# A Mamba block between two ternary FFNs on one core: the first pass's silu from a tanh on ScalarE and a product on VectorE

## What is computed

```
x = x + 0.5 * ffn(layernorm(x))       # ffn: ternary weights times their mean absolute value, plus a bias
x = x + mamba(layernorm(x))
x = x + 0.5 * ffn(layernorm(x))       # the same weights

mamba(x):
  u, z  = split(x @ W_in.T)           # 1024 features each
  u     = silu(causal convolution of u along the tokens, 4 taps, plus conv_b)
  x_dbl = u @ W_xproj.T               # 64 columns for dt, 16 for B, 16 for C
  dt    = softplus(x_dbl[:, :64] @ W_dt.T + b_dt)
  h[t]  = exp(dt*A) * h[t-1] + dt * B[t] * u[t]      # 16 states a feature, A = -exp(A_log)
  y     = sum over states of h*C + u * Dskip
  out   = (y * silu(z)) @ W_out.T
```

## Time and profile before

| | us |
|---|---|
| median of 3 runs (2982.8 to 2990.77) | 2988.41 |
| the profiled execution | 2993.49 |
| its span in the trace | 2991.6 |
| first pass in it (the second pass's first load is at 1093.77) | about 1094 |
| DVE busy / PE busy / ACT busy over the span | 2483.3 / 2457.8 / 1943.3 |

### The profile page before, as it was taken

How to read it: one execution, slowest core, us unless ns; L and a number is a source line. 1 busy time by engine, 2 the same in 40 slices (tenths; PEclk the granted TensorE clock), 3 DMA queues, 4 the chain that set the end, 5 groups by cost and what they waited for, 6 DMA issues and landing times.

```text
span 2991.6 us, 42858 instructions
## 1 busy us (share of the span) xinstructions
PE 2457.8 (82%) x12448; PEld 1413.9 (47%) x12448; DVE 2483.3 (83%) x3261; ACT 1943.3 (65%) x3457; POOL 1921.5 (64%) x1705
## 2 busy tenths in 40 slices
PE   3577999899998726788889888888888888889887
PEld 1233444444443315555555555555555555555553
DVE  5565666767666649999999999999999999999991
ACT  2233766756765666677777767767777767777772
POOL 1112222222221138899989989989989989999983
PEclk8788999999998857799999999999999999999998
DMA  5454233233232263352352352353352352343330
GB/s 206 155 205 168 78 128 135 78 128 121 92 128 107 79 214 117 92 131 69 112 132 68 99 140 74 99 132 82 98 133 76 102 135 72 106 119 87 105 76 35
DMA packets 175016, 337.66 MB, mean 113 GB/s; under 512 B 41696, under 2 KB 91104, under 8 KB 174496
## 3 DMA queue, kind: packets, MB, share of 16 engines
q1 hardware_dynamic: 160928, 284.23, 28.8%
q0 software_dynamic: 13824, 50.34, 8.8%
HBM read 174.61 MB, written 109.58 MB: 95 GB/s over the span
## 4 chain that ended last, share of the span: by engine, by line
POOL 28%; DVE 13%; issue 12%; PE 5%; DMA 3%; ACT 1%; POOLq 1%; SPq 0%; DVEq 0%; ACTq 0%
POOL dbu L1055 22%; DVE h L1279 9%; DVE y L1292 3%; PE p_g L1402 2%; PE p_g L1411 1%; PE p_ht L1368 1%; POOL o L1100 1%; DMA y<-y_part 1%; POOL carry L1066 1%; POOL y L1075 1%; POOL y L1090 1%; POOL x L1094 1%; DMA dt_<-dt_scratch 1%; POOL dbu L1060 1%; DMA dtu_<-dtu_scratch 1%
## 5 line engine op out<-in xcount | busy, mean ns | idle before, releaser
L1279 DVE TENSOR_TENSOR_SCAN h<-p_da,dbu 128x512 f32<-128x512 f32 x1024 | 1189.0, 1206 | 44.7 <-ACT p_da L1161 21.9
L1055 POOL TENSOR_TENSOR dbu<-dtu_,bb 128x1024 f32<-128x1024 f32 x512 | 1205.3, 2385 | 4.7 <-DMA dtu_<-dtu_scratch 4.1
L1161 ACT ACTIVATE p_da<-dt_,neg_a 128x255 f32<-128x255 f32 x2048 | 886.5, 467 | 400.3 <-DVE h L1279 377.5
L1368 PE MATMUL p_ht<-ident,h 128*128 128x128 f32 x4096 | 596.6, 305 | 157.9 <-DVE h L1279 156.7
L1368 PEld LDWEIGHTS p_ht<-ident,h 128*128 128x128 f32 x4096 | 534.6, 159 | 250.5 <-issue 111.2
L1292 DVE SCALAR_TENSOR_TENSOR y<-p_ht,ct,y 128x1024 f32<-128x1024 f32 x400 | 505.9, 1265 | 4.9 <-PE p_ht L1368 4.8
L714 PE MATMUL p_u<-xz,wu 128*128 128x512 f16 x1536 | 351.4, 386 | 10.8 <-DVE xz L508 9.2
L1402 PE MATMUL p_g<-wo,tokt 128*128 128x512 f16 x1536 | 355.2, 389 | 1.6 <-ACT tokt L1193 1.6
L70 POOL TENSOR_TENSOR small<-small,consts 128x1 f32<-128x1 f32 x96 | 71.1, 740 | 441.4 <-DVE small L63 441.4
L1411 PE MATMUL p_g<-wz,xz 128*128 128x512 f16 x1536 | 345.2, 381 | 0.0
L363 POOL TENSOR_TENSOR late<-dt,u 128x512 f32<-128x512 f32 x64 | 81.7, 1276 | 378.0 <-DVE dt L561 378.0
(11 more groups left out here) (120 smaller groups left out, 3053.7 us busy)
## 6 DMA issues: line engine op xcount, KB each, us to landing
y<-y_part POOLq DMA_DIRECT2D x96, 512.0 KB, 5.8
bb<-b_scratch SPq DMA_DIRECT2D x128, 256.0 KB, 3.5
xin<-in_x SPq DMA_DIRECT2D x32, 512.0 KB, 5.5
x_scratch<-x SPq DMA_DIRECT2D x32, 512.0 KB, 4.8
xz_scratch<-xz SPq DMA_DIRECT2D x16, 1024.0 KB, 6.0
y_scratch<-late SPq DMA_DIRECT2D x32, 512.0 KB, 5.1
dt_scratch<-dt SPq DMA_DIRECT2D x64, 256.0 KB, 2.1
dtu_scratch<-late SPq DMA_DIRECT2D x64, 256.0 KB, 2.4
```

The source lines that it names most:

```text
L1055: nc.gpsimd.tensor_tensor(state[:, 4 * f:4 * f + 4, :], dtu[:, 4 * f:4 * f + 4, :], bb[n // NB % 2][:, n % NB:n % NB + 1, :].to_broadcast( ...
L1161: ins_ = nc.scalar.activation(p_da[p % 2][:, k * T2 + 1:(k + 1) * T2], dt[:, g, 1:], ACT.Exp, scale=neg_a[:, g, n:n + 1])
L1279: nc.vector.tensor_tensor_scan(h[n % 2][:, 2 * p:2 * p + 2, :].rearrange("p g t -> p (g t)"), p_da[p % 2][:], dbu[n % 2][:, 2 * p:2 * p + ...
L1368: mm = nc.tensor.transpose(p_ht[t][:, g * P:(g + 1) * P], h[n % 2][:, g, t * P:(t + 1) * P], ident[:])
```

## The change

In the first pass `silu` becomes two instructions. ACT computes tanh(acc/2) (`half_tanh`) into the `up` buffer, which the convolution of this group has read. DVE then forms (tanh + 1) * acc = 2 * silu(acc) (`twice_silu`) into u. So u holds twice its value, and this is taken out elsewhere: the evacuation of x_dbl gets a per-partition scale from a small tile `halves` (0.5 for dt and C, 0.25 for B, since dt*u is doubled too), and Dskip is halved once. `half_tanh` stands in ACT's list where `silu` stood. `twice_silu` of group 2j-1 stands in DVE's list ahead of s phase 0, that of group 2j ahead of s phase 2. `u_work` of a group now waits for the product of the group two before it, where it waited for its convolution, since the tanh lies in `up`.

```
-                def silu(i, par, g):
+                def half_tanh(i, g):
                     q = i * G + g
                     wait(act, conv_done, q + 1)
-                    if g == 0:
-                        wait(act, dtu_done, (i - 1) * G)
-                        b, m = unit_at(i - 2, "y", G - 1)
-                        wait(act, s_full[b], m)
-                    nc.scalar.activation(u[par][:, g, :], acc[g % 2][:], ACT.Silu).then_inc(silu_done, 1)
+                    nc.scalar.activation(up[g % 2][:, 3:3 + T1], acc[g % 2][:], ACT.Tanh, scale=0.5).then_inc(th_done, 1)
...
-                    wait(act, conv_done, q - 1)
+                    wait(act, silu_done, q - 1)
                     nc.scalar.activation(up[g % 2][:, 3:3 + T1], p_u[g % 2][:], ACT.Copy,
...
-                            nc.scalar.activation(xdbl[:], p_s[v % 2][0:R + 2 * NS, :], ACT.Copy).then_inc(s_free[v % 2], 1)
+                            if isinstance(d, int) and d == 0:
+                                act.wait_ge(halves_set, 2)
+                            nc.scalar.activation(xdbl[:], p_s[v % 2][0:R + 2 * NS, :], ACT.Copy, scale=halves[:]
+                                                 ).then_inc(s_free[v % 2], 1)
...
                     nc.scalar.mul(half_bias[:], half_bias[:], 0.5).then_inc(const_done, 1)
+                    nc.scalar.mul(dskip[:], dskip[:], 0.5).then_inc(dskip_halved, 1)
...
+                def twice_silu(i, par, g):
+                    q = i * G + g
+                    wait(dve, th_done, q + 1)
+                    if g == 0:
+                        wait(dve, dtu_done, (i - 1) * G)
+                        b, m = unit_at(i - 2, "y", G - 1)
+                        wait(dve, s_full[b], m)
+                    nc.vector.scalar_tensor_tensor(out=u[par][:, g, :], in0=up[g % 2][:, 3:3 + T1], scalar=1.0,
+                                                   in1=acc[g % 2][:], op0=ALU.add, op1=ALU.mult).then_inc(silu_done, 1)
...
+                    nc.vector.memset(halves[:], 0.5).then_inc(halves_set, 1)
+                    dve.wait_ge(halves_set, 1)
+                    nc.vector.memset(halves[R:R + NS, :], 0.25).then_inc(halves_set, 1)
...
                         row_stats(dve, nc, x1[j % 2], stats[1], mv[1], vn[1], small[:, 41:42], ln_chain[1], stats_ready[1],
                                   scale_ready[1], k)
+                    if had_u(i, j):
+                        twice_silu(i if j else i - 1, par if j else 1 - par, (2 * j - 1) % G)
                     w_work(i, j, slice(0, 2))
                     if s_on:
                         s_work(d, 1 - par, j, 0)
...
                     w_work(i, j, slice(2, None))
+                    if u_on:
+                        twice_silu(i, par, 2 * j)
                     if s_on:
                         s_work(d, 1 - par, j, 2)
```

More of the change, by code:

```diff
@@ L119, in first_pass @@
         xdbl = sb("xdbl", [R + 2 * NS, T1])
+        halves = sb("halves", [R + 2 * NS, 1])
         ct = sb("ct", [P, TT1, NS])
@@ L141, in first_pass @@
         const_loaded, const_done = sem("const_loaded1"), sem("const_done1")
+        dskip_halved, halves_set = sem("dskip_halved"), sem("halves_set")
         ident_step, ffn_loaded = sem("ident_step"), [sem(f"w_ffn_loaded{i}") for i in range(4)]
@@ L161, in first_pass @@
         u_full, up_done, conv_chain, conv_done = sem("u_full"), sem("up_done"), sem("conv_chain"), sem("conv_done")
-        silu_done = sem("silu_done")
+        th_done, silu_done = sem("half_tanh_done"), sem("silu_done")
         s_full = [sem(f"s_full{i}") for i in range(2)]
@@ L482, in step @@
                     if had_u(i, j):
-                        silu(before[0], par if j else 1 - par, before[1])
+                        half_tanh(*before)
                     w_high(i, j, slice(0, 2))
@@ L496, in step @@
                     if u_on:
-                        silu(i, par, 2 * j)
+                        half_tanh(i, 2 * j)
                     if s_on:
@@ L541, in s_work @@
                             if isinstance(d, int) and d == 0:
+                                dve.wait_ge(dskip_halved, 1)
                                 for b in range(2):
```

## The result

The changed kernel takes 3027.09 us in the median of four runs (3023.58 to 3028.98), the one before 2989.59 (2982.8 to 2990.8): a ratio of 1.0129, 95% interval 1.011 to 1.0147. The sign was forecast; the size was not: 18 us were predicted and 37 measured, and 3027.09 lies just above the upper end of the range, 3026.

What follows compares the result with a forecast made beforehand. The prediction took PE plus its stalls on ACT's and DVE's queues as the bound. Its terms (15.6 - 3.0 - 8.4 + 12.0 + 1.1 + 0.6) gave +17.9 us on 2988.4, so 3006 us, range 2985 to 3026.

Steps and rivals of the forecast that it cites:

- Loads and products: First pass: 36 table loads go from ACT, 46.2 us; 64 products come onto DVE, 48.1 us.
- Unit x: PE's unit x in step 0 starts late, its product queued behind DVE's statistics: 2.6 us a chunk, +15.6 us.
- the clock: PE's clock changes around longer or shorter stalls: kept out of the sum, -6 to +12 us in the range.
- Rival 4: Clock falls at the new stalls at x and in step 2, none given back in step 1: 3018 us, chance 0.10.
- Step 3 into 0: At d7 DVE's waits for Exp and Ln go, a product takes their place: -0.5 us a chunk, -3.0 us.
- Step 1: The load ahead of d0's Exp goes, so `up`, convolution and low halves come earlier: -1.4 us a chunk, -8.4 us.
- Step 2: The product waits for tanh at the head of DVE's queue, delaying d2 and the convolution: +2.0 us a chunk, +12.0 us.
- PE's wait of 4.4 us at the turn: Sign to look for in step 2: PE's wait of 2.48 us at the turn grows to near 4.4 us.
- Setup and end: Halving Dskip delays the first FFN, +1.1 us; in the end part gains and losses meet, 0 (-3 to +4).
- Rival 1: Tanh gets a table of its own in the first pass, so no load goes: 3018 us, chance 0.06.
- 2 and 3: Rivals: only ACT's chain matters, 2970 us, chance 0.14; slack absorbs x's delay, step 2 cancels step 1, 2993 us, 0.15.
- a switch of 2.66 us: Skill's rule for a table switch with its drain; it would give 2998 us; the prediction used 1.28 us instead.

Runs made afterwards that it cites:

- e7: Kernel before, silu kept, plus an equally long unused DVE product at the two places, waiting only for the convolution: ratio 1.0007.
- e6: Kernel before with one added wait: in step 0 ACT's silu of group 7 waits for the statistics of x1: ratio 1.0077.
- e5: e3 plus Dskip's halving behind the ternary weights and the product of group 2j behind s phase 3: ratio to the kernel before 0.9992.
- e8: Kernel before with one added wait: in steps 1 to 3 DVE waits for the silu of group 2j-1 ahead of s phase 0: ratio 1.0058.
- e4: Changed kernel with silu's function in place of tanh, so its table loads return (u's values are wrong): ratio to the kernel before 1.0203.
- e1: Changed kernel with group 7's product in step 0 moved ahead of the statistics of x1 on DVE: ratio to the kernel before 1.0068.
- e3: Changed kernel with the moves of both e1 and e2: ratio to the kernel before 0.9997.
- e2: Changed kernel with the product of group 2j-1 in steps 1 to 3 moved behind s phase 0 on DVE: ratio to the kernel before 1.0057.

## Why the prediction was right in sign and wrong in size

- *Loads and products:* right, 28 loads for Exp and 35 for tanh (36 forecast), 64 products of 0.7 us, for whose amount no cost can be told (e7). The scaled evacuation of x_dbl takes 685 ns in place of 594, as forecast.
- *Unit x:* the delay was right: 2.1 us a chunk were forecast with the gain of step 3 taken off (2.6 - 0.5), and step 3 and step 0 up to x together are 2.06 longer in the mean of five. What the sum left out is the clock: the stretch behind x costs 2.2 us more in the mean (1.78 in the chunk shown), and the 16 matmuls take 9.42 in place of 7.09 us, which is 14 us over the six chunks. e6 has the late x alone and measured 23 us in place of 15.6. **This is the step that failed**: the clock "is not in the sum". It stood only in the range, as -6 to +12, with half of the loss set against half of a gain. (The range given for the sum, 2998 to 3016, is not quite 3006 with these bounds, which is 3000 to 3018.)
- *Rival 4* had the clock's fall at x, but said that none is given back in step 1, and some is: there the FFN of step 2 takes 7.07 us in all five periods, where it took 7.55 to 8.97 before. In step 2 the fall that it expected was largely there already: the turn took 1.94 us in four of the five periods before and does so in all five after. Its 3018 us is still 9 short.
- *Step 3 into 0:* -0.5 predicted. In chunk 4 it is -0.78, but +0.05 in the mean of five, so the gain can't be read from step 3 alone; it is in the net above.
- *Step 1:* -1.4 predicted, -1.95 in the mean. The load gives 1.28, the turn ahead of the FFN about 0.6: it runs in 1.10 to 1.16 us where it took 1.26 to 1.94 before, so the clock came back here.
- *Step 2:* mechanism and place right (convolution 1.9 us later against 2.0), but the term is too small: +3.01 in the mean, +3.69 in the chunk shown. 0.9 of it is the first tap beside POOL's product, which the sum did not look at: **the second step that failed**, 5 to 6 us over the six chunks. The 0.6 us that the turn is longer in chunk 4 (1.94 against 1.34) is that chunk's alone. Of the signs, the convolution without idle time came true; PE's wait of 4.4 us at the turn did not, since PE meets the delay at y5.
- *Setup and end:* +1.1 and 0 predicted, 2.5 and 1.9 measured. The 2.5 is no finding: the same FFN starts between 260.83 and 265.12 us in the traces that keep the silu, and at 267.05 after. The first FFN of all starts at 35.45 where these have 33.02 to 33.51, so something of 1 to 2 us is there, and the Dskip move did not clearly remove it in the time (e5).
- *Rival 1* falls by the count of loads, and 2 and 3 fall by the time itself and by e6 and e8, which show that neither delay is taken up by slack.
- *The cited rules:* a switch of 2.66 us (the Trainium skill, ScalarE: Activation LUTs, "What ACT_TABLE_LOAD costs") is not borne out: 64 loads of 1283 ns have 1.1 us idle before them in all, and step 1 gained 1.95 us with a clock's part in it. The placement rule (the Trainium skill, ScalarE activation tables: per-element evaluation and per-set limits, "Table sets in the compiler and the runtime") led to the right answer on tanh and Exp, which share one load; Exp behind an Ln still took a load each time, 28 in all.

The forecast of 2.7 us a period against 5.32 measured is thus 2.2 of clock at x and 1.0 in step 2, less 0.5 that step 1 gave more. The stretches of a trace always add up to its period, so this says where the time lies and not why. It does not close as a sum of ratios: e6 and e8 give 1.35 points, e4 takes back 0.74 and e7 adds 0.07, which makes 0.7 and not 1.3. The product's own 0.7 us in the queue of step 2 belongs to the gap; the rest stays open. That the two places are the whole loss rests on e1 to e3.

## What to carry over

When a function is split over two engines, the new second half takes a place in a queue, and the place can cost far more than the length: here 46 us of work cost nothing that could be told from noise, a wait ahead of ready work 17 us, and one late operand of a PE unit 23. List what stands behind the new wait and ahead of the new instruction, and put the instruction behind whatever is ready. A stall that is added to PE ahead of a long unit is to be priced with the clock of the unit, by the nearest rows at both levels, and a mean of several periods is worth more than one.

## What the runs showed of the hardware

- A wait of PE of 2.9 to 3.8 us ahead of unit x was followed by 16 matmuls in 8.7 to 10.1 us in the changed kernel (clock 0.90 in the stretch of one), a wait of 0.7 to 2.0 us by 7.1 (e1, e3). Not always: in e4 x took 7.11 us behind a wait of 3.09 and 8.80 behind one of 2.66. In the six places each of the changed kernel, e2, e4 and e6 the waits were 2.3 to 3.9 us, and 22 of the 24 units took 8.67 us or more. Behind waits of up to 2.2 us, in all other traces, they took 7.0 to 7.1 us in these places.
- The first tap, a fp32 TENSOR_SCALAR from SBUF of 0.55 us, takes longer when a large POOL product runs as it starts, and in every such row of these traces it ends 0.27 to 0.30 us behind that product: 1.43 us where POOL's 1.26 us over 128x512 began 0.11 us ahead of it (changed kernel, e1, e4, e8), 2.53 us where 2.35 us over 128x1024 began 0.10 us ahead, which is in the kernel before too, late in the pass:

```profile
916.52 2.35 POOL L374 TENSOR_TENSOR x<-xin,half_bias 128x1024 f32<-128x1024 f32 x1
916.62 2.53 DVE L519 TENSOR_SCALAR acc<-up,conv_w,conv_b 128x512 f32<-128x512 f32 x1
```

- The later taps kept 0.75 us, but POOL's product had ended before they started, so they show nothing of this. The product of tanh and acc, a SCALAR_TENSOR_TENSOR from SBUF of 0.69 us, was lengthened too: 0.97 us in e2 (692.98), where POOL's 1.27 us had begun at 692.13. DVE's two low halves, with one operand in PSUM, kept 1.28 us for both (711.42 in the changed kernel) while a POOL product ran from 711.59 to 712.86.
